# A third expert's values sent through the output projection before they are weighted

## The reference, cut to what matters

```python
h = tok(x)                                     # 16 x 36 x 192
h = layernorm(h + attention(h))
gate = softmax(relu(h @ Wg1 + bg1) @ Wg2 + bg2)
top_w, top_i = top_k(gate, 2); top_w = softmax(top_w)
for e in range(3):
    ve = h @ Wv[e] + bv[e]                     # 36 x 64 for each image
    att = einsum(q[e], k[e]) * scale           # e == 2: + pos_bias
    att = softmax(where(future, -inf, att))
    ys[e] = att @ ve
combined = concat(ys[e] * w_e[e])              # 36 x 192 for each image
h = layernorm(h + combined @ Wp + bp)
```

## Time and profile before

| | |
|---|---|
| median of 3 runs | 118.58 us (118.58, 113.70, 118.98) |
| profiled execution | 113.86 us, of which the span of its instructions 111.7 us |
| TensorE granted clock | 0.995 of full speed |
| busy: PE, PEld, DVE, ACT, POOL | 90%, 80%, 70%, 64%, 27% |

### The profile page before, as it was taken

One profiled execution on the slowest core, in us unless ns is written; L12 is line 12 of the kernel. 1 busy time (PEld: TensorE's weight loads), 2 busy tenths in 40 slices (PEclk: granted clock), 3 DMA queues, 4 the chain that ended last, 5 costly groups with the idle time before them and its releaser, 6 DMA issues.

```text
span 111.7 us, 3468 instructions
## 1 busy us (share of the span) xinstructions
PE 100.1 (90%) x1349; PEld 89.8 (80%) x1349; DVE 78.5 (70%) x239; ACT 71.1 (64%) x198; POOL 30.1 (27%) x42
## 2 busy tenths in 40 slices
PE   6989999999999999999999999999959868797940
PEld 4778998998998889789988998998948767684910
DVE  0566909955991887319686888988867779988670
ACT  4678687577659965976865558662366366558260
POOL 4003626699914500000591630000005400000000
PEclk9999999999999999999999999999999999999997
DMA  3999999300000000000000000000000000000202
GB/s 75 355 336 387 414 421 426 126 0 0 6 3 6 3 6 0 0 6 0 0 0 6 0 6 0 0 6 0 3 0 6 3 0 0 6 0 0 65 20 79
DMA packets 4123, 7.73 MB, mean 69 GB/s; under 512 B 1292, under 2 KB 2444, under 8 KB 3980
## 3 DMA queue, kind: packets, MB, share of 16 engines
q1 hardware_dynamic: 3740, 7.24, 17.8%
q10 hardware_dynamic: 368, 0.28, 0.8%
HBM read 7.08 MB, written 0.44 MB: 67 GB/s over the span
## 4 chain that ended last, share of the span: by engine, by line
PE 61%; DVE 16%; ACT 7%; DMA 5%; issue 5%; SPq 3%; DVEq 0%; ACTq 0%
PE proj L920 11%; PE outp L1050 8%; PE score L1005 7%; DMA x_f<-x_t 5%; PE proj L905 4%; PE trans L1029 3%; PE outp L884 3%; PE proj L909 3%; PE proj L906 3%; PE proj L912 3%; PE proj L913 3%; PE proj L1067 2%; ACT ln_ln L562 2%; DVE ln_st L733 2%; PE proj L1072 1%
## 5 line engine op out<-in xcount | busy, mean ns | idle before, releaser
L548 ACT ACTIVATE pt_t<-trans,image_t 108x216 f32<-108x216 f32 (+1 forms) x42 | 14.5, 420 | 1.4 <-PE trans L1029 1.3
L424 POOL TENSOR_TENSOR h_res<-h_hi,bias 128x288 f32<-128x288 f32 x8 | 5.2, 666 | 23.3 <-DVE h_lo L757 23.2
L532 ACT ACTIVATE score<-d_t 128x296 f32<-128x296 f32 (+2 forms) x16 | 6.5, 409 | 6.2 <-DVE d_t L697 6.1
L1005 PE MATMUL score<-k_t,q_t 64*36 64x37 f32 (+1 forms) x416 | 10.3, 196 | 0.0
L1005 PEld LDWEIGHTS score<-k_t,q_t 64*36 64x36 f32 x416 | 9.0, 111 | 1.2 <-issue 0.6
L707 DVE TENSOR_REDUCE sm_t<-score 128x8 f32<-128x288 f32 (+1 forms) x16 | 6.9, 434 | 2.8 <-ACT score L532 2.8
L726 DVE TENSOR_TENSOR x_lo<-outp,x_hi 128x288 fp32r<-128x288 f32 x12 | 5.4, 452 | 4.9 <-ACT x_hi L555 4.8
L694 DVE TENSOR_REDUCE mx_t<-score 128x8 f32<-128x296 f32 (+2 forms) x16 | 7.1, 444 | 2.4 <-PE score L1013 1.4
L920 PE MATMUL proj<-wv_hi,h_hi 128*108 128x384 f32 (+1 forms) x24 | 8.3, 344 | 0.2 <-DVE wv_hi L659 0.2
L562 ACT ACTIVATE ln_ln<-ln_mv,const 108x1 f32<-108x1 f32 (+1 forms) x12 | 3.5, 293 | 7.3 <-DVE ln_mv L736 7.3
L651 DVE TENSOR_TENSOR x_lo<-x_f,x_hi 128x288 fp32r<-128x288 f32 x12 | 6.8, 580 | 1.8 <-ACT x_hi L464 1.8
(11 more groups left out here) (192 smaller groups left out, 335.7 us busy)
## 6 DMA issues: line engine op xcount, KB each, us to landing
ffn_f<-f_w SPq DMA_DIRECT2D x1, 1088.0 KB, 12.1
wqk_f<-w_qk SPq DMA_DIRECT2D x2, 512.0 KB, 7.9
x_f<-x_t SPq DMA_DIRECT2D x2, 432.0 KB, 6.3
wv_f<-w_v SPq DMA_DIRECT2D x1, 768.0 KB, 7.1
wo_f<-w_out SPq DMA_DIRECT2D x1, 768.0 KB, 9.5
x_f<-x_t SPq DMA_DIRECT2D x2, 288.0 KB, 4.8
tw_f<-tok_w SPq DMA_DIRECT2D x2, 256.0 KB, 4.3
wqk_f<-w_qk SPq DMA_DIRECT2D x2, 256.0 KB, 5.6
```

The lines of the kernel that those rows point to most:

```text
L548: nc.scalar.activation(pt_t[:, n % 2, 0:tiles, :, i], trans[0:ROWS, 0:tiles, :, 0:TOK], ACT.Copy, scale=image_t[:, i:i + 1]).then_inc(spli ...
L1005: ins = nc.tensor.matmul(s[64 * h:64 * h + TOK, im, 0:width], q, k_t[rows, n % QK_RING, im, 0:width], start=(kind == "attn" and im == 0), ...
```

## The change

For expert 2 the values v (72 or 108 tokens by 64 features) are transposed by TensorE (`ft g`), copied into `third_t` (`fe g`, ACT), multiplied by the weights in plain float32 (`vp g z`, three matmuls of 192 columns) and copied into `third_p` (`vc g z`, ACT). `out2 g t` is then one plain float32 matmul of the probabilities with `third_p`. The upper 64 rows of `third_t` are zero, from a memset on GpSimd. Gone are `pv 13`, `pv 15`, `oh 13`, `oh 15`, `ol 13`, `ol 15` and the two F32R matmuls of the old `out2` for each tile. The three lists are written anew throughout, also where nothing else changed.

```diff
@@ new functions of TensorE
+            def third_turned(g):
+                b = take("ft", g)
+                pe.wait_ge(fv_s, max(fv_order.index((g, z)) + 1 for z in range(2)))
+                for j in range(TILES):
+                    rows = tile_rows(j)
+                    ins = nc.tensor.transpose(b[0:128, tile_cols(j)], fv_t[0:rows, TILES * g + j, HD:DIM],
+                                              ident[0:rows, 0:rows])
+                ins.then_inc(projected, 1)
+
+            def third_out(g, z):
+                b = take("vp", (g, z))
...
+                pe.wait_ge(third_s, g + 1)
+                for n, j in enumerate(FV_TILES[z]):
+                    ins = nc.tensor.matmul(b[0:tile_rows(j), DIM * n:DIM * n + DIM], third_t[:, g, tile_cols(j)],
+                                           ffn_f[:, 1, F_PROJ:F_PROJ + DIM], start=True, stop=True)
+                ins.then_inc(projected, 1)
+
+            def add_third(g, t):
...
+                pe.wait_ge(third_p_s, third_order.index((g, z)) + 1)
+                pe.wait_ge(split, splits_through(n - 1) + (3 if t < 2 else 4))
+                probs = pt_t[0:rows, n % 2, t, 0].rearrange("p i t -> p (i t)")[:, 0:rows]
+                nc.tensor.matmul(b[0:rows, 0:DIM], probs, third_p[0:rows, TILES * g + t], start=False, stop=True,
+                                 skip_group_check=True).then_inc(summed, 1)
@@ new functions of ScalarE
+            def third_features(g):
+                act.wait_ge(projected, ready[("ft", g)])
+                nc.scalar.activation(third_t[HD:128, g], bank("ft", g)[HD:128, 0:GT], ACT.Copy).then_inc(third_s, 1)
+
+            def third_projected(g, z):
+                act.wait_ge(projected, ready[("vp", (g, z))])
...
+                nc.scalar.activation(third_p[0:rows, TILES * g + first:TILES * g + first + count], src,
+                                     ACT.Copy).then_inc(third_p_s, 1)
@@ the list of TensorE, its part on group 1's first products and on the end
+v 0 0, qk 2, em 10, em 11, qk 3, v 0 1, t 0, s 2, s 3, v 0 2, qk 4, t 1, v 1 0, s 4, pv 0, pv 1
...
+outa 1 2, outb 1 2, qk 12, tr 1, qk 13, s 12, s 13, gate 1, ft 0, lg 1, vp 0 0, vp 0 1, t 12, qk 14
+fv 1 0, qk 15, fv 1 1, s 14, pv 12, s 15, t 13, ft 1, vp 1 0, vp 1 1, res2 0 0, t 14, res2 0 1, one2 0 0
+res2 0 2, one2 0 1, out2 0 0, one2 0 2, out2 0 1, t 15, out2 0 2, pv 14, tr2 0, res2 1 0, one2 1 0
+res2 1 1, out2 1 0, one2 1 1, out2 1 1, res2 1 2, one2 1 2, out2 1 2, tr2 1
```

More of the change, by code:

```diff
@@ L93, in halved @@
     return ENTRIES[n][0::2] == LAST
+VALUED = [n for n in range(len(ENTRIES)) if not halved(n)]
 def half_image(h, i):
@@ L112 @@
-outa 1 2, outb 1 2, qk 12, tr 1, qk 13, s 12, gate 1, s 13, lg 1, qk 14, qk 15, t 12, fv 1 0, s 14, pv 12
-s 15, t 13, fv 1 1, pv 13, res2 0 0, res2 0 1, t 14, one2 0 0, res2 0 2, one2 0 1, out2 0 0, out2 0 1
-one2 0 2, out2 0 2, t 15, pv 14, tr2 0, pv 15, res2 1 0, one2 1 0, res2 1 1, one2 1 1, out2 1 0, out2 1 1
-res2 1 2, one2 1 2, out2 1 2, tr2 1
+em 11, qk 3, v 0 1, t 0, s 2, s 3, v 0 2, qk 4, t 1, v 1 0, s 4, pv 0, pv 1, t 2, qk 5, t 3, qk 6, pv 2
+pv 3, s 5, s 6, t 4, v 1 1, v 1 2, t 5, qk 7, pv 4, pv 5, s 7, qk 8, outa 0 0, t 6, outb 0 0, outa 0 1
@@ L209, in vit_tower @@
             "p (g c t) -> p g c t", g=GROUPS, c=2) for t in (tw_hi, tw_lo))
+        third_t = sb("third_t", [128, GROUPS, GT])
+        third_p = sb("third_p", [ROWS, GROUPS * TILES, DIM])
         h_res = sb("h_res", [128, GROUPS, NCH, GT])
@@ L273, in vit_tower @@
         fv_order = [w[1:] for w in DVE_STEPS if w[0] == "cf"]
+        third_order = [w[1:] for w in ACT_STEPS if w[0] == "vc"]
         norms = [(w[0][2:], w[1], w[2]) for w in DVE_STEPS if w[0] in ("ap", "ap2")]
@@ L315, in vit_tower @@
                 plan("fv", key, (fv_s, fv_order.index(key) + 1))
+            elif kind == "ft":
+                plan("ft", key, (third_s, key + 1))
+            elif kind == "vp":
+                plan("vp", key, (third_p_s, third_order.index(key) + 1))
             elif kind == "lg":
@@ L401, in _ @@
             pool.memset(edges[:], 0.0).then_inc(zeroed, 1)
+            pool.memset(third_t[0:HD], 0.0).then_inc(zeroed, 1)
             pool.memset(wgt_last[:], 0.0).then_inc(zeroed, 1)
-            pool.wait_ge(zeroed, 4)
+            pool.wait_ge(zeroed, 5)
             pool.memset(g1_t[32:33], 1.0).then_inc(zeroed, 1)
@@ L535, in split_transposed @@
                 act.wait_ge(transposed, n + 1)
-                if n >= 2:
-                    act.wait_ge(attended, n - 1)
+                if n >= 2 and halved(n - 2):
+                    act.wait_ge(summed, max(sums.index(("2", ENTRIES[n - 2][1], t)) for t in range(TILES)) + 1)
+                elif n >= 2:
+                    act.wait_ge(attended, VALUED.index(n - 2) + 1)
                 if n == 0:
@@ L571, in split_h1 @@
                     nc.scalar.activation(hcols(h_hi, g, c), bank("tr", (g, c))[:, 0:GT], ACT.Copy).then_inc(h1_hi_s, 1)
+            def third_features(g):
[3 more added lines that the diff above has]
+                act.wait_ge(projected, ready[("vp", (g, z))])
+                first, count, rows = FV_TILES[z][0], len(FV_TILES[z]), tile_rows(FV_TILES[z][0])
+                src = bank("vp", (g, z))[0:rows, 0:count * DIM].rearrange("p (j d) -> p j d", d=DIM)
+                nc.scalar.activation(third_p[0:rows, TILES * g + first:TILES * g + first + count], src,
+                                     ACT.Copy).then_inc(third_p_s, 1)
             def copy_result(g):
@@ L623, in _ @@
                     gate_hidden(*a)
+                elif kind == "fe":
+                    third_features(*a)
+                elif kind == "vc":
+                    third_projected(*a)
                 elif kind == "ge":
@@ L1167, in _ @@
                     expert_values(*a)
+                elif kind == "ft":
+                    third_turned(*a)
+                elif kind == "vp":
+                    third_out(*a)
 def kernel(**inputs):
```

89 lines of the change are left out of this document (46 added, 43 removed).

## The result

| | before | after |
|---|---|---|
| median of 20 runs, alternating on one chip | 113.92 us (113.43 to 118.98) | 114.52 us (113.84 to 116.25) |
| profiled execution | 113.86 us, span 111.7 | 114.14 us, span 112.1 |
| mean granted TensorE clock of it | 0.995 | 0.992 |

After over before is 1.0055, with a 95% interval of 1.0035 to 1.0075: 0.6 us slower, where the prediction gave 119.2 us for 118.58. The ratios of this document are taken from undisturbed executions; four of the twenty of the kernel before lay above 117 us, two of them among the three whose median was 118.58. With more runs that kernel is at 113.9.

The account below looks back on a forecast made before the run. PE bounds 30 to 73.5 us, then a back-and-forth chain sets the end. Stages +0.2, back to −0.1, +0.2, +0.6, +0.2 then +0.6 gave +0.6 us: median 118.58 to 119.2, range 113.0 to 120.4.

Parts of the forecast that it names:

- the term of 4.72 us: Gap between the profiled execution (113.86 us) and the median of the runs shown (118.58), carried over whole into the forecast.
- The float32 price: PE: a plain float32 matmul of 192 columns costs 0.32 us, bounds 0.19 and 0.42.
- C: Rival, chance 0.13: faster by over 2%, float32 matmul at 0.19 us, with the smaller gain rival: −2.3 us.
- Early, +0.2: First projection: PE waits 0.4 us for `xs 11` before `em 11`; net +0.2 us, bounds −0.3 and +0.5.
- the two signs by which I said I would be wrong: PE waits in a new place before 73 us, or `sp 13` isn't held by `fe 1`.
- First norm of group 1, −0.1: Group 1's first norm on DVE: last tile's statistics earlier, 0.3 us gained, back to −0.1; `tr 1` at 83.0.
- Gate, +0.2: Group 1's gate: exponential on ACT delayed behind `vc 0 0`, +0.2 us; scores of entry 14 at 94.0, not 93.8.
- Second norm of group 0, +0.6: Group 0's second norm: first `out2` tile ends at 100.85 us, where the statistics started at 100.20; +0.6.
- `sp 13` stands behind `fe 1` on ACT: ACT before group 0's second norm: `sp 13` starts at 97.65 us instead of 96.32.
- End of group 1: First tile of group 1's second norm +0.2 us (105.7), last tile another +0.4 (107.1), waiting for PE; +0.6 in sum.
- A: Rival, chance 0.25: ACT queue waits don't arise, `fe 1` finds `ft 1` done; 0.5 to 1.1 us faster.
- B: Rival, chance 0.12: ACT's queue bounds from the gate on, `fe 1` ending after 98.1; 2.3 us or more slower.

Follow-up runs that it names:

- the kernel with the old start: Changed kernel with all three lists of the kernel before up to group 1's first norm, new lists from there on: ratio to before 1.0118.
- the runs with zeros: Products of zeros in PE's waits: kernel before 1.0071, changed kernel 1.0106, changed kernel with old beginning 1.0114; ahead of the bank wait: before 0.9992, changed 1.0058.
- the run with own banks: Changed kernel with group 1's first two `out2` tiles in PSUM banks outp0 and score0, their residuals ahead of `tr2 0`: ratio to before 1.0038.
- the old lists: New computation in the lists of the kernel before, new steps put in at the nearest places: ratio to before 1.0568, 6.5 us slower.
- Moving the values alone: New computation in the lists of the kernel before, with `fv 1 1` and `cf 1 1` moved early: ratio to before 1.0339, 117.76 us.
- the first trial: Kernel before with products of zeros in PE's waits of group 1, those at the first norm's transposes behind the wait for the bank: ratio 1.0071.
- the pair above: Changed kernel (1.0055, clock stayed up) and the same with only group 0's third expert by the new path (1.0102, clock fell): like PE waits before 89 us.
- a run whose clock fell: Computation of the kernel before with the new lists: ratio to before 1.0025 (0.9992 to 1.0057).

## Why the prediction was right and wrong

**The time: wrong, by one step.** Forecast were 119.2 us, measured 114.52, which lies within the stated range of 113.0 to 120.4 but 4.7 us below the time. The step that failed is the term of 4.72 us between the profiled execution and the median of three runs. It read: "the lowest run, 113.70, is beside it; no row tells what the 4.72 us are, so I carry them over whole". The sum against the profiled execution, 114.5 us, is what was measured (median 114.52, ratio 1.0055, that is +0.6), in part by luck, as the stages below show. What I added to it was the distance to two runs of a kind that comes about once in seven. The runs with a clock on record show what they are: of the kernel before, every run at 117 us or more had a mean clock of 0.932 to 0.952, all others 0.969 or more. A mean of 0.97 to 0.98 means nothing for this kernel's time: 49 such runs have a median of 113.8 us, the 51 at 0.985 or more 113.9. In several traces the clock falls only behind the last products (near 108.1 us with `out2` in F32R), where little but transfers is left. The text saw both readings, and with a profile at 113.86 beside a run of 113.70 and a clock of 0.995, the profile's side was the one to take.

**The float32 price: right.** 0.34 us for each of the `vp` products where I took 0.32, in two records each. That excludes C, which needed 0.19. The Trainium skill (FP8 and Floating Point Precision, TensorE Precision Notes) has four passes for true FP32; by four F32R rows that was 0.36, as near as my 0.32, and the trace still shows two records and not four. In F32R `out2` is worth 0.4 us in all, and the last tile's statistics start 0.7 us earlier (1.1 us counted from the transposes), where I had 0.4 for the later one.

**Early, +0.2: wrong, there is no such wait.** `em 11` did not wait. `xs 11` was done in time, for DVE ran 0.4 us ahead (`sh 0` at 18.73, not 19.1) and the split took 0.45 us, not the 0.69 I had read from another one. PE got a new wait of 0.21 us for wqk_lo at 21.15 instead. That was one of the two signs by which I said I would be wrong, and it is a small one: the last tile of the first projection starts at 79.82 in the changed kernel and at 79.78 in the one before. What moved the kernel with the old start to 1.0118 is the clock in the stretch that follows, by the runs with zeros, and for the clock I had not looked at all.

**First norm of group 1, −0.1: right in kind.** PE's idle time before the transposes is 0.96 us in every trace of the new start and 1.19 or 1.20 in those of the old one, zeros aside. Their time (82.91 for 83.10, predicted 83.0) lies within the scatter of such starts and proves nothing.

**Gate, +0.2: twice as large, and on another path.** DVE waits for the exponential behind `vc 0 0` (0.19 us at 90.20), as said, and its convolution of entry 14 ends 0.23 us later than before. But the scores of entry 14 do not wait for it any more. PE is busy without a break from 90.31 to 96.7 and reaches them at 94.22, behind `fv 1 1`, where 93.80 was before and 94.0 predicted. I let `vp 0` (1.06 us) and `fv 1 1` fill PE's gaps at no cost; they fill them to the brim, and PE's queue is now what ends last. Besides, the queries' products wait 0.19 us for the bank that `vc 0 0` frees (90.31). `vc 0 1` did have room: the queries' copy behind it waits 0.41 us for PE.

**Second norm of group 0, +0.6: the size right, by luck in the split.** Forecast 100.85, measured 100.84, with `sp 13` at 97.72 for 97.65. But of the 0.64 us against before, 0.6 arise between the transposes and the scores of entry 14 (11.31 us for 10.70) and 0.2 behind them (6.62 for 6.40), with the transposes 0.2 earlier; I had 0.3 and 0.45. And the bold step, "`sp 13` stands behind `fe 1` on ACT", is a fact of the order and not a cost: put ahead, it makes the norm 0.3 us later. The holder is the chain that I named second. `ft 1` waits for the values; then come `fe 1`, 1.03 us of `vp 1` in float32, and PE's queue behind it, which has no idle time from 97.84 on; DVE waits 0.21 us for `out2 0 0` at 100.84. DVE's wait of 0.52 us for `ex 15` at 99.48 ends earlier and is not the last. That `vp 1` in F32R would give part of it back is not shown: the run that had it left out part of the product, and its clock fell.

**End of group 1: right in kind.** The first tile was to come 0.2 us later than before and the last 0.6. They came at 105.45 (predicted 105.7, before 105.52) and 106.84 (107.1, 106.48), and the last one waits for PE as forecast. From the first statistics of group 0 to the last of group 1 the change wins 0.28 us (6.00 for 6.28), where I had none. The span of the profiled execution grew by 0.4 us, the median by 0.6. The run with own banks confirms that PE's queue is what the last tile waits for.

**The rivals.** A (0.5 to 1.1 us faster) needs `fe 1` to find `ft 1` done; it waited 0.80 us. B needed `fe 1` after 98.1; it ended at 97.70. With the old lists its sign does show, `fe 1` at 101.79 and the time 6.5 us longer, but not its mechanism: ACT is idle for 3.10 us there and waits for the values, and the clock is low twice. Moving the values alone wins 2.4 of the 6.5 us. That the lists are written anew is no side matter, it is what makes the new path nearly free.

**What stays open.** I did not see a trace of an execution of the kernel before at 117 us or more; that its clock is low in the stretch where other kernels have it low is by analogy. That PE's idle time brings the fall is supported by the zeros and not proven. At 15% (21 of 137), twelve runs without one at 117 come by chance in one case of seven (0.85 to the twelfth is 0.14), and with the six of the first trial in one of twenty; that only one of the twelve is below 0.98 in mean clock, where 66 of 117 were, says more. Against idle time as the sole cause stands the pair above: the same waits, and the clock fell in one execution and not in the other. And the exact split of the 0.6 us between lists (0.3, with an interval from below zero, in a run whose clock fell) and path is within the measurement. Why one issue of SyncE takes 0.8 us longer in two of the kernels is open.
